# Three accumulation tables instead of five for the scatter-adds of a four-layer graph network

## The reference, cut to what matters

```python
agg = zeros((12500, 64))
agg = agg.at[src].add(edge_attr_64)    # src in any order
agg = agg.at[dst].add(edge_attr_64)    # dst is sorted
h = relu(concat([x, agg], 1) @ W1 + b1)
x = layernorm(x + h @ W2 + b2)
```

## Time and profile before

| | |
|---|---|
| median of 3 runs | 16361.84 us |
| lowest and highest | 16351.66, 16367.62 us |
| profiled execution, its span from first to last instruction | 14902.1 us |
| its busy time on POOL | 11248.6 us (75%) |
| on PE | 6227.2 us (42%) |
| on DVE | 5856.8 us (39%) |
| on ACT | 1515.3 us (10%) |
| mean granted clock of PE | 0.611 |

### The profile page before, as it was taken

How to read it: one execution, slowest core, us unless ns; L and a number is a source line. 1 busy time by engine, 2 the same in 40 slices (tenths; PEclk the granted TensorE clock), 3 DMA queues, 4 the chain that set the end, 5 groups by cost and what they waited for, 6 DMA issues and landing times. The chain is left out here.

```text
span 14902.1 us, 144289 instructions
## 1 busy us (share of the span) xinstructions
PE 6227.2 (42%) x24247; PEld 4729.8 (32%) x24274; DVE 5856.8 (39%) x23264; ACT 1515.3 (10%) x5955; POOL 11248.6 (75%) x9886
## 2 busy tenths in 40 slices
PE   1666666666666666540000000000355555555556
PEld 0444444444444444320000000000244344434443
DVE  4333333333333333442222222222355555555554
ACT  2000000000000000230000000000011111111111
POOL 3888888888888888537777777777777777777775
PEclk9666667767666666775555555555555555555555
DMA  5444444444444444432222222222122222222221
GB/s 167 62 62 62 62 62 62 62 62 62 62 62 62 62 62 62 105 135 66 66 65 66 66 65 66 65 65 66 40 65 66 66 65 66 66 65 66 66 65 37
DMA packets 1277375, 1014.71 MB, mean 68 GB/s; under 512 B 733185, under 2 KB 1134226, under 8 KB 1276577
## 3 DMA queue, kind: packets, MB, share of 16 engines
q0 software_dynamic: 670640, 300.26, 17.3%
q1 hardware_dynamic: 606704, 714.11, 14.8%
HBM read 451.20 MB, written 562.28 MB: 68 GB/s over the span
## 5 line engine op out<-in xcount | busy, mean ns | idle before, releaser
L108 POOL DMA_INDIRECT table<-sums,row_i x3125 | 4856.5, 1554 | 969.7 <-issue 881.2
L102 POOL DMA_INDIRECT msg<-Y,idx x3125 | 2951.4, 944 | 1049.9 <-issue 952.0
L102 POOL DMA_INDIRECT yg<-ytab,idx x3125 | 2949.9, 944 | 962.6 <-issue 936.5
L494 PE MATMUL ps<-ident,meta 128*128 128x128 f32 x6260 | 1531.2, 430 | 2433.5 <-ACT meta L468 2433.5
L494 PEld LDWEIGHTS ps<-ident,meta 128*128 128x128 f32 x6260 | 1347.6, 321 | 2519.5 <-ACT meta L468 2519.5
L1009 DVE SCALAR_TENSOR_TENSOR run<-run,same,msg 128x64 f32<-128x64 f32 x3125 | 896.3, 287 | 3010.6 <-DMA msg<-Y,idx 2921.1
L625 PE MATMUL ps<-tail,before 128*128 128x80 f32 (+2 forms) x6 | 2.0, 426 | 3964.7 <-PEq L935 3915.5
L568 DVE TENSOR_TENSOR row_i<-route,meta 128x5 int32<-128x5 f32 x625 | 103.5, 166 | 3484.2 <-DMA table<-sums,row_i 3484.2
L1402 DVE SCALAR_TENSOR_TENSOR run<-run,same,ps 128x32 f32<-128x32 f32 x3125 | 774.7, 248 | 1548.2 <-PE ps L1307 1452.3
L625 PEld LDWEIGHTS ps<-tail,before 128*128 128x128 f32 x6 | 1.5, 310 | 3965.4 <-issue 3965.4
L496 PE MATMUL ps<-upper,ident 128*128 128x512 f32 x1252 | 1129.0, 1003 | 0.0
(11 more groups left out here) (234 smaller groups left out, 8715.4 us busy)
## 6 DMA issues: line engine op xcount, KB each, us to landing
R<-run SPq DMA_DIRECT2D x625, 200.0 KB, 1.9
R<-run SPq DMA_DIRECT2D x626, 160.0 KB, 1.8
v<-in_edge_attr SPq DMA_DIRECT2D x625, 160.0 KB
R<-run SPq DMA_DIRECT2D x390, 256.0 KB, 2.1
Y<-tab SPq DMA_DIRECT2D x98, 512.0 KB, 2.7
table<-sums,row_i POOLq DMA_INDIRECT x3125, 3.1
msg<-Y,idx POOLq DMA_INDIRECT x3125, 2.4
Z<-zeros SPq DMA_DIRECT2D x125, 400.0 KB, 2.8
```

Source lines behind the costliest of these rows:

```text
L102: eng.indirect_dma_start(out=out, out_offset=None, in_=table, in_offset=bass.IndirectOffsetOnAxis(ap=index, axis=0)).then_inc(sem, 16)
L108: eng.indirect_dma_start(out=table, out_offset=bass.IndirectOffsetOnAxis(ap=index, axis=0), in_=in_, in_offset=None, **kw).then_inc(sem, 16)
L494: nc.tensor.matmul(ps[:, t * P:(t + 1) * P], meta[:, q, 0, t:t + 1].to_broadcast([P, P]), k.ident[:, :], start=t in (0, 4), stop=False)
```

## The change

The five tables become three. Tile `t` goes to table `t % 3`, so that a slot's tiles go to tables 0, 1, 2, 0, 1. `SHARE` = [2, 2, 1] is how many scatter-adds of a slot a table gets. Every wait counts by these shares. The waits of ACT and DVE before a buffer is written again now name all three tables and the slot five back, in place of the last table and the slot four back. Setup fills, and `nodes_01` loads and adds, three tables.

```diff
-NTAB = SL
+NTAB = 3
+SHARE = [len(range(a, SL, NTAB)) for a in range(NTAB)]
...
 # ACT, ahead of the copy to sums, and DVE, ahead of row_i
-                        act.wait_ge(added[NTAB - 1], 16 * (n - NS + 2))
+                        for a in range(NTAB):
+                            act.wait_ge(added[a], 16 * SHARE[a] * (n - NS + 1))
...
 # POOL
                     for t in range(SL):
-                        if not (is_first(c) and q == 0):
-                            hold(pool, added[t], 16 * n, k.passed)
-                        scatter(pool, k.tables[t], row_i[:, q, t:t + 1], sums[:, q, t, :], added[t], add=True)
+                        a, before = t % NTAB, t // NTAB
+                        if before or not (is_first(c) and q == 0):
+                            hold(pool, added[a], 16 * (SHARE[a] * n + before), k.passed)
+                        scatter(pool, k.tables[a], row_i[:, q, t:t + 1], sums[:, q, t, :], added[a], add=True)
...
-            for t in range(SL):
-                pool.wait_ge(added[t], 16 * SLOTS)
+            for a in range(NTAB):
+                pool.wait_ge(added[a], 16 * SHARE[a] * SLOTS)
```

More of the change, by code:

```diff
@@ L566, in body @@
                     if not is_first(c):
-                        v.wait_ge(added[NTAB - 1], 16 * (n - NS + 2))
+                        for a in range(NTAB):
+                            v.wait_ge(added[a], 16 * SHARE[a] * (n - NS + 1))
                     v.tensor_tensor(row_i[:, q, :], route[:, q % 2, :], meta[:, q, 0, :], ALU.add).then_inc(row_ready, 1)
```

## The result

The changed kernel takes 16567.35 us (median of 4 runs, 16549.56 to 16593.82) against 16356.75 us (median of 4) for the kernel before beside it: ratio 1.013, 95% interval 1.0116 to 1.0145, some 210 us more. The direction was forecast, at +120 us; the time lies just above the range, which ended at 16560.

The account below looks back on a forecast made before the run. POOL's first-layer scatter-adds, 1.859 us a tile, were taken to bound their stretch, 39% of the span. Stalls +130 us, setup -8 and `nodes_01` -2 gave +120 us on 16362: 16482 us, range 16395 to 16560 us.

Parts of the forecast that it names:

- The distance: Scatter-adds to one table: tiles 0 and 1 follow at distance two, 3.72 us; tiles 3 and 4 at three, 5.58 us.
- What a release costs: POOL's wait on a register's value: 0.81 us from release to DMA start, not overlapping the DMA that runs.
- The rival of a free release: Release overlaps POOL's running DMA, so tile 0 is not late; only savings remain, 16352 us; chance 0.11, free or nearly.
- A landing after 3.10 us: Scatter-add start to landing, 3.1 us in the middle; with 0.81 us release, tile 0 starts 0.19 us late.
- 3.0 to 3.2 at the ends: Spread of scatter-add landings; as bounds on the stall, 3.0 us gives 56 us and 3.2 us gives 180 us.
- Tile 1 ... asks for the same lateness and not for more: Tile 1 waits for tile 4, one step after tile 3; the later landing decides, adding some 0.02 us.
- gaps twice a slot: Sign of being wrong in POOL's scatter-adds: two gaps a slot would mean tile 1 has a lateness of its own.
- some 620 idle times put down to a landing: Sign expected in the changed profile: POOL idle about 0.5 us ahead of a scatter-add, one a slot.
- A stall here is not won back: In POOL's scatter-add stretch a late tile shifts all that follow; 620 slot ends of 0.21 us give 130 us.
- Setup: 8 of 20 zero fills go, so the search's gathers share less: 8 us won, bounds nothing to 15 us.
- `nodes_01`: 28 of 70 loads and adds go: 2 us won in the first group, nothing in the other 13, hidden under PE.
- The 1460 us outside the trace: Median of runs over the profiled span, unexplained by the trace; the change was added to it unchanged.

Follow-up runs that it names:

- two kernels: Against the kernel before: four tables, no distance below three, 14907.48 against 14899.69 us; three tables in a strict cycle, every distance three, 14939.22 against 14895.92 us.
- the kernel with a distance of one: Kernel before with its five tables, but tile 0 waits for tile 4 of the slot before: 18003.55 us (one run) against 16654.49 us.
- the cyclic kernel: Kernel before with three tables in a strict cycle, three turns joined, ACT and DVE waiting on one semaphore: 14939.22 against 14895.92 us, ratio 1.0025.

## Why the prediction was wrong, point by point

- **What bounds the stretch**: right. POOL alone; ACT and DVE stay slots ahead (waits of up to 10.1 and 7.1 us for landings).
- **The distance**: right, by the experiments. Distance three costs nothing (two kernels), distance two costs a stall for each place where it stands (all of them +224 us, tile 0's alone +159 us, two a turn in place of ten +74 us), distance one costs 1333 us.
- **"What a release costs", 0.81 us**: right. Landing to start is 0.79 us in the changed kernel's trace, with POOL still busy, and the kernel with a distance of one, where POOL is idle, fits the same figure. The rival of a free release is out. The Trainium skill (DMA: Bandwidth & Descriptors, "Anatomy of one DMA") has some 50 ns for the sequencer's dispatch; the traces here, with 0.79 us, don't agree with that as the whole way from a met wait to the start.
- **"A landing after 3.10 us"**: a term mis-sized. It came from one profiled execution. The same kernel profiled again gave 3.2 us, and 3.17 us is what the changed kernel's trace gives from tile 3's start to the landing that tile 0 waits for, in the median. Where 0.19 us is the difference of 3.91 and 3.72, 0.07 us more is a third of it: tile 0 costs 0.242 x 624 = 151 us, not 0.19 x 620 = 118. The bound taken, landing at 3.2 us, allowed for it.
- **"3.0 to 3.2 at the ends"**: the earlier trace rows was read as all tiles, but it lacks tile 1, which lands some 0.65 us later (3.75 us). It did no harm, by luck: the change has tile 4 wait for tile 1, at a distance of three. A short distance behind tile 1 would have cost 3.75 + 0.79 - 3.72 = 0.82 us a slot, some 510 us, an estimate from these figures.
- **"Tile 1 ... asks for the same lateness and not for more"**: this step failed. It got 0.02 x 620 = 12 us, for the spread of two landings, and cost 68 us. The spread is a small part: 16 us are in the ordinary steps, as expected, and 52 us in pauses of 0.7 and 1.3 us of POOL's sequencer between a wait that is met and the DMA behind it, a term that the prediction did not have. One of its own signs of being wrong, gaps twice a slot, asked for this. Its other sign in the profile, some 620 idle times put down to a landing, did not come: they stand under "issue". In the first pause shown, the semaphore instruction of tile 1 is recorded at 2238.33 us, 0.02 us behind the landing, and its scatter-add starts at 2240.43 us, 2.10 us later in place of 0.79.
- **"A stall here is not won back"**: right, but half of the thought. The distance did not only hide landings. In the kernel before, the semaphore instruction for the scatter-add that starts at 3010.14 us passes at 3003.99 us: the sequencer was three DMAs ahead, and a pause of 1.3 us vanished in that. The short distance took this lead away, for tile 1 most of all, which waits second. With tile 1's wait moved back to five, the pauses fell where there is cover; at a distance of three the wait is met 2.4 us ahead (1.5 us behind a tile 1), and of the 3,124 steps none is over 2.3 us in the one kernel, and one in the other. The kernel before has the same pauses: behind tile 4's wait, where 0.52 us is the rule, its sequencer's records have 1.23 us in 11 places, 280 scatter-adds apart, and 1.85 us in 5 places, 545 apart, at the same tiles in both of its profiles. No step of either profile is over 2.3 us.
- **Setup**: 8 us forecast, 7.4 measured (and 326.9 against 319.1 and 319.0 in the other profiles). **`nodes_01`**: the adds went from five to three in the first group, 3.26 to 1.94 us; the block as a whole is not measurably shorter. From the last scatter-add to the first gather of `edges_2` are 426, 420 and 417 us in three profiles with five tables and 417 us in two with three, at the level of 14900 us; a gain of 0 to 2 us is below that spread.
- **The 1460 us outside the trace**: wrong reading, harmless for the sum. They were the level of the batch, as above.

The sum with measured terms: +151 + 68 - 7 - 1 = +211 us, against 210.6 us measured (the last term is not measured but taken from the adds of the first group). Range and chances held the sign; the range was too narrow on the side of the unforeseen term. The sum had 118 us for tile 0 and 12 us for tile 1; they cost 151 and 68 us.

The row for the first group's adds in the changed kernel, which answers to the earlier trace rows:

```profile
6371.39 1.94 DVE L893 TENSOR_TENSOR cat<-cat,tabs 128x448 f32<-128x448 f32 x3
```

What stays open: what the pauses are (they go with the DMAs issued; no run changed the DMAs' number or size), why tile 1 lands late, whether a wait on a plain number in the loop, 0.28 us in the earlier trace rows, would hide stall and pauses at a distance of two (not tried), and the more frequent low clock in `nodes_01` of the cyclic kernel.

## What to carry to other kernels

Buffers that are rotated to hide a DMA's landing must be judged at the shortest distance in the pattern, not by their mean number: three tables are enough for the scatter-adds when they are in a strict cycle and too few when a slot of five breaks it. The distance must cover the landing and the release behind it (here 3.2 + 0.8 us against steps of 1.86), for each place in the loop on its own, since one place can land later than the others (here 4.0 + 0.8 us), and a margin on top, since the lead of the sequencer is what hides its rare pauses; a wait that is met just in time exposes them. And a duration from one profile, of which a small difference is taken, needs its spread between executions in the range.

## What the runs showed of the hardware

POOL, with a wait on a register's value ahead of an indirect DMA, starts it 0.79 us after the landing, idle or busy. Its sequencer pauses for 1.3 us at every 109th or 110th scatter-add and for 0.7 us at every 55th to 58th, where the records let it be seen, at the same tiles in each execution of a kernel. Scatter-adds of one size at one place in the loop landed 4.03 us after their start, those at the four others 3.18 to 3.20 us. Landings of the same scatter-adds (without tile 1's) in the same kernel had a median of 3.10 us in one execution and 3.18 us in another. And the same kernel took 14900, 16357 or 16654 us in different batches; the changed kernel's scatter-adds took the same time to 2 us at 16567 and at 16855 us.
